# Linear attention: squares move from VectorE to ScalarE, the maxima are taken per half, and ScalarE's order in the queries' pass is new

## The reference

```python
def softmax_kernel_features(data, proj, is_query):
    d = data.shape[-1]
    data_normalizer = 1.0 / math.sqrt(math.sqrt(d))
    ratio = 1.0 / math.sqrt(proj.shape[0])
    data_dash = jnp.einsum('bhnd,md->bhnm', data_normalizer * data, proj)
    diag_data = jnp.sum(jnp.square(data), axis=-1, keepdims=True) * 0.5 * data_normalizer * data_normalizer
    if is_query:
        stab = jnp.max(data_dash, axis=-1, keepdims=True)
    else:
        stab = jnp.max(data_dash)
    return ratio * (jnp.exp(data_dash - diag_data - stab) + EPS)
...
q1 = softmax_kernel_features(q, proj_mat, is_query=True)
k1 = softmax_kernel_features(k, proj_mat, is_query=False)
kv = jnp.einsum('bhnm,bhnd->bhmd', k1, v)
ksum = jnp.sum(k1, axis=2)
z = 1.0 / jnp.einsum('bhnm,bhm->bhn', q1, ksum)
out = jnp.einsum('bhnm,bhmd->bhnd', q1, kv) * z[..., None]
```

## Time and profile before

| | us |
|---|---|
| Median of 3 runs | 2392.24 |
| Lowest and highest | 2391.66, 2395.35 |
| The profiled execution: its span, from the first to the last instruction | 2403.1 |
| TensorE busy in it | 1879.3 (78%) |
| VectorE busy | 1495.5 (62%) |
| ScalarE busy | 1074.7 (45%) |
| Keys' pass, first transposes to last VectorE pass | 147.2 to 255.1 |
| Queries' pass, first products to last VectorE pass | 330.6 to 529.1 |

### The profile page before, as it was taken

One profiled execution on the slowest core, in us unless ns is written; L12 is line 12 of the kernel. 1 busy time (PEld: TensorE's weight loads), 2 busy tenths in 40 slices (PEclk: granted clock), 3 DMA queues, 4 the chain that ended last, 5 costly groups with the idle time before them and its releaser, 6 DMA issues. The chain is left out here.

```text
span 2403.1 us, 30974 instructions
## 1 busy us (share of the span) xinstructions
PE 1879.3 (78%) x9780; PEld 1007.5 (42%) x9804; DVE 1495.5 (62%) x2518; ACT 1074.7 (45%) x1896; POOL 395.9 (16%) x595
## 2 busy tenths in 40 slices
PE   3868788858876453777668877998899984999994
PEld 2745655535333320000022234442133333888883
DVE  4558449966010687999878876999788883111114
ACT  1100222214110476999979964342477661222220
POOL 5000000000112010222100003331033343222221
PEclk8989999968887575555589978997799996999997
DMA  3011110005797004443011008777666703566664
GB/s 85 1 39 31 48 31 27 20 10 229 309 411 314 20 0 127 127 127 123 18 32 40 26 16 119 130 132 107 83 88 95 97 28 135 195 201 203 202 203 184
DMA packets 147792, 264.98 MB, mean 110 GB/s; under 512 B 28864, under 2 KB 115985, under 8 KB 142678
## 3 DMA queue, kind: packets, MB, share of 16 engines
q1 hardware_dynamic: 135750, 242.10, 38.0%
q0 software_dynamic: 10768, 18.19, 2.3%
q10 hardware_dynamic: 1152, 3.15, 0.3%
HBM read 221.85 MB, written 57.71 MB: 116 GB/s over the span
## 5 line engine op out<-in xcount | busy, mean ns | idle before, releaser
L1743 PE MATMUL ps<-arena 128*128 x376 | 194.9, 621 | 108.2 <-ACT ps L1785 60.1
L1785 ACT ACTIVATE ps<-ps,arena 128x512 f32<-128x512 f32 x384 | 256.7, 1121 | 6.3 <-POOL arena L1769 6.3
L1753 DVE TENSOR_REDUCE arena<-ps 128x1024 f32 x192 | 232.8, 1225 | 24.5 <-PE ps L1743 12.2
L1785 ACT ACTIVATION_READ_ACCUMULATOR ps<-ps,arena 128x1 f32 x384 | 234.7, 668 | 0.0
L2159 DVE TENSOR_REDUCE arena<-ps 128x1024 f32 x192 | 221.3, 1219 | 12.4 <-PE ps L2405 9.8
L2618 ACT ACTIVATE arena<-ps 128x1024 f32<-128x1024 f32 x192 | 185.1, 1020 | 97.6 <-PE ps L2500 96.4
L2962 DVE TENSOR_TENSOR arena<-ps,arena 128x384 f32<-128x384 f32 x39 | 21.8, 558 | 286.4 <-PE ps L2918 286.4
L2942 ACT ACTIVATE arena<-ps,arena 128x256 f32<-128x256 f32 x234 | 89.5, 481 | 235.9 <-PE ps L2907 230.0
L2405 PE MATMUL ps<-arena 96*128 96x512 bf16 x500 | 162.7, 430 | 26.4 <-DVE arena L2159 12.2
L1950 ACT ACTIVATE arena<-ps 128x1024 f32<-128x1024 f32 x192 | 178.7, 1048 | 7.8 <-DVE arena L1970 4.6
L529 PE MATMUL ps<-arena 96*128 96x456 f32 (+1 forms) x512 | 170.3, 482 | 8.8 <-DMA arena<-la_xt 5.2
(11 more groups left out here) (394 smaller groups left out, 3264.8 us busy)
## 6 DMA issues: line engine op xcount, KB each, us to landing
arena<-in_sm_w_dram SPq DMA_DIRECT2D x128, 576.0 KB, 15.5
arena<-in_re_w_dram SPq DMA_DIRECT2D x39, 1252.0 KB, 5.9
arena<-ra_parts SPq DMA_DIRECT2D x192, 192.0 KB, 9.1
routed_in<-routed_in SPq DMA_DIRECT2D x8, 3332.0 KB, 14.2
ra_parts<-arena SPq DMA_DIRECT2D x48, 192.0 KB, 2.4
arena<-routed_in SPq DMA_DIRECT2D x39, 196.0 KB, 5.4
arena<-la_xt SPq DMA_DIRECT2D x16, 384.0 KB, 3.4
arena<-arena SPq DMA_DIRECT2D x64, 96.0 KB, 2.2
```

The source lines that it names most:

```text
L1743: ins = pe.matmul(ps[:, 2 * (n % 4) + t % 2, :], QM[j][:, h, t * P:(t + 1) * P], KI[:, b, h // HG, :], start=True, stop=True)
L1753: v.tensor_reduce(MXq[:, b, 2 * u:2 * u + 2, at_head(h)], ps[:, 2 * (n % 4):2 * (n % 4) + 2, :], AX.X, ALU.max).then_inc(s_lk, 1)
L1785: ins = act.activation(bank, bank, ACT.Exp, bias=nb[n % 4][:, t % 2:t % 2 + 1], scale=c_reg, accum_out=RS[:, b, t, at_head(h):at_head(h) + 1])
```

## The change

VectorE's copy and product are left out in both passes. ScalarE squares the 192 numbers straight from PSUM into `SQ` (`square`), and VectorE sums what it wrote. A semaphore per pass (`ks`, `qs`) tells VectorE that the square is there. The maximum is taken in two instructions, one for each bank: first over bank 1, then, after the wait for the square, over bank 0 from which ScalarE reads the 192 numbers. In the keys' pass ScalarE's list is now squares of tiles 0 and 1, the copy of the next batch's turned rows, squares of tiles 2 and 3. In the queries' pass it is rewritten: square of t, exponential of t-1, copy of t-1. Before, it had the exponential of t and then the copy of t-1. TensorE's and SyncE's lists are as before.

```diff
-    MX = g2(P, [B, T])
+    MX = g2(P, [B, T, 2])
...
+    def square(act, b, t, product, done):
+        product.wait(act, b, t + 1)
+        act.activation(SQ[t % 2], ps[:, 2 * (t % 2), 0:D], ACT.Square).then_inc(done.sem, 1)
+
     def squared_lengths(v, link, t):
-        q = ps[:, 2 * (t % 2), 0:D]
-        link(v.tensor_copy(SQ[t % 2], q))
-        link(v.tensor_tensor(SQ[t % 2], SQ[t % 2], q, ALU.mult))
         link(v.tensor_reduce(dg[t % 2], SQ[t % 2].rearrange("p (h d) -> p h d", h=NH), AX.X, ALU.add))
+    one_group = lambda t, g: ps[:, 2 * (t % 2) + g, D:D + FH]
...
                 for t in range(T):
                     kp.wait(v, b, t + 1)
+                    largest = lambda g: v.tensor_reduce(MX[:, bass.ds(b, 1), t, g], one_group(t, g), AX.X, ALU.max)
+                    largest(1)
+                    ks.wait(v, b, t + 1)
+                    largest(0)
                     squared_lengths(v, link, t)
-                    v.tensor_reduce(MX[:, bass.ds(b, 1), t], features(t), AX.XYZ, ALU.max)
...
+            turned(0, 0, 0)
+            with act.Fori(0, B // 2 - 1) as i:
                 for j in range(2):
-                    b = 2 * i + j
-                    xt.wait(act, b, 1)
-                    prev(act, kp, i, j)
-                    act.wait_ge(s_xs[j], 16 * i + 1)
-                    act.activation(XTs[j], ps[0:DC, 4:6, :], ACT.Copy).then_inc(xc.sem, 1)
+                    squares(2 * i + j, (0, 1))
+                    turned(2 * i + j + 1, i + j, 1 - j)
+                    squares(2 * i + j, (2, 3))
...
                 qp.wait(v, b, t + 1)
-                q = ps[:, 2 * j, 0:D]
-                v.tensor_copy(SQ[j], q)
-                link(v.tensor_reduce(mq[j].rearrange("p (g h) -> p g h", g=2), features(t), AX.X, ALU.max))
-                link(v.tensor_tensor(SQ[j], SQ[j], q, ALU.mult))
-                link(v.tensor_reduce(dg[j], SQ[j].rearrange("p (h d) -> p h d", h=NH), AX.X, ALU.add))
+                largest = lambda g: v.tensor_reduce(mq[j][:, 6 * g:6 * g + 6],
+                                                    one_group(t, g).rearrange("p (h f) -> p h f", h=6), AX.X, ALU.max)
+                largest(1)
+                qs.wait(v, b, t + 1)
+                largest(0)
+                squared_lengths(v, link, t)
...
+            def batch(b, i, j, behind):
+                square(act, b, 0, qp, qs)
+                if behind:
+                    exp(b - 1, T - 1)
+                    turned(b - 1, 1 - j, T - 1)
+                prev(act, num, i, j)
+                for t in range(1, T):
+                    square(act, b, t, qp, qs)
+                    exp(b, t - 1)
+                    turned(b, j, t - 1)
```

More of the change, by code:

```diff
@@ L545, in linear_attention @@
         S1("k_products", T, T + 1), S1("k_features", T, 2)
+    ks = S1("k_squares", T, 2)
     s_lk, s_mx, s_gm, s_ns = (sem(f"la_{n}") for n in ("k_chain", "row_max", "global_max", "guard_ready"))
@@ L563, in batch @@
             def batch(b, ahead):
-                link = Link(v, s_lk, b * (3 * T))
+                link = Link(v, s_lk, b * T)
                 for t in range(T):
                     kp.wait(v, b, t + 1)
+                    largest = lambda g: v.tensor_reduce(MX[:, bass.ds(b, 1), t, g], one_group(t, g), AX.X, ALU.max)
+                    largest(1)
+                    ks.wait(v, b, t + 1)
+                    largest(0)
                     squared_lengths(v, link, t)
-                    v.tensor_reduce(MX[:, bass.ds(b, 1), t], features(t), AX.XYZ, ALU.max)
                     v.scalar_tensor_tensor(
@@ L580, in _ @@
             kd.wait(v, B - 1, T)
-            v.tensor_reduce(gmax, MX, AX.XY, ALU.max).then_inc(s_mx, 1)
+            v.tensor_reduce(gmax, MX, AX.XYZ, ALU.max).then_inc(s_mx, 1)
             v.wait_ge(s_gm, 1)
@@ L592, in _, with turned, squares @@
             xc.start(act)
+            ks.start(act)
             for j in range(2):
                 act.sem_inc(s_xs[j], 1)
-            with act.Fori(0, B // 2) as i:
-                for j in range(2):
-                    b = 2 * i + j
-                    xt.wait(act, b, 1)
-                    prev(act, kp, i, j)
-                    act.wait_ge(s_xs[j], 16 * i + 1)
-                    act.activation(XTs[j], ps[0:DC, 4:6, :], ACT.Copy).then_inc(xc.sem, 1)
+            def turned(b, i, j):
+                xt.wait(act, b, 1)
+                prev(act, kp, i, j)
+                act.wait_ge(s_xs[j], 16 * i + 1)
+                act.activation(XTs[j], ps[0:DC, 4:6, :], ACT.Copy).then_inc(xc.sem, 1)
+            def squares(b, some):
+                for t in some:
+                    square(act, b, t, kp, ks)
+            turned(0, 0, 0)
+            with act.Fori(0, B // 2 - 1) as i:
+                for j in range(2):
+                    squares(2 * i + j, (0, 1))
+                    turned(2 * i + j + 1, i + j, 1 - j)
+                    squares(2 * i + j, (2, 3))
+            squares(B - 2, (0, 1))
+            turned(B - 1, B // 2 - 1, 1)
+            squares(B - 2, (2, 3))
+            squares(B - 1, range(T))
         @block.sync
@@ L771, in linear_attention @@
         S1("q_turned", T, 2), S1("q_turned_copied", T, 2)
+    qs = S1("q_squares", T, 2)
     num, ot, pr, hh = S1("read_out", 2, 3), S1("normalised", 2), S1("projected"), S1("stream_updated")
@@ L826, in batch @@
             def batch(b, behind, last_behind):
-                link = Link(v, s_qk, b * (4 * T))
+                link = Link(v, s_qk, b * (2 * T))
                 chain(b, link, 0)
@@ L849, in _, with exp, turned @@
         def _(act):
-            for s in (qe, qc):
+            for s in (qe, qc, qs):
                 s.start(act)
-            with act.Fori(0, B // 2) as i:
-                for j in range(2):
[L854 to L864, removed]
+            def exp(b, t):
+                qd.wait(act, b, t + 1)
+                act.activation(QD[t % 2], QD[t % 2], ACT.Exp).then_inc(qe.sem, 1)
+            def turned(b, j, t):
+                qt.wait(act, b, t + 1)
+                act.activation(Q1T[j][:, :, t * P:(t + 1) * P].rearrange("p (g a) q -> p g a q", g=2),
+                               ps[0:2 * NF, 4:6, 0:3 * P].rearrange("p g (a q) -> p g a q", a=3),
+                               ACT.Identity, bias=little[0:2 * NF]).then_inc(qc.sem, 1)
+            def batch(b, i, j, behind):
[8 more added lines that the diff above has]
+                    turned(b, j, t - 1)
+            batch(0, 0, 0, False)
+            batch(1, 0, 1, True)
+            with act.Fori(1, B // 2) as i:
+                for j in range(2):
+                    batch(2 * i + j, i, j, True)
+            exp(B - 1, T - 1)
+            turned(B - 1, 1, T - 1)
         @block.tensor
```

## The result

The changed kernel takes 2382.8 us (median of 7 runs, 2379.4 to 2386.9) beside 2392.7 us for the kernel before (7 runs): ratio 0.9949, 95% interval 0.9937 to 0.9962. By the medians it is faster by 9.9 us, where 9.1 were forecast; by the ratio, which takes in all runs, it is 12 us (9 to 15). In two later groups of runs, on two chips, the same kernel stood at 0.9932 (0.9909 to 0.9956) and 0.9932 (0.9909 to 0.9954), which is 16 us by the ratio and 17.0 and 17.7 us by the medians. The three intervals overlap, so it is not shown that the gain differs from group to group. The forecast held in the comparison for which it was made; what the traces show that it did not have comes further down.

A forecast was written before the change was run, and what follows sets the result against it. A chain between TensorE and VectorE bounds the keys' round, VectorE the queries' pass. Gains of 8.2 us (keys) and 0.9 us (queries) sum to 9.1, from a median of 2392.24 to 2383.1 us; 8 in 10 range 2377.5 to 2391.

The forecast's parts named there:

- The chain: Keys' pass: links between TensorE and VectorE set the round, 12.73 us before and 11.71 us after.
- VectorE's 1.95 us: Keys' pass: VectorE's work on a tile, from data to the next instruction, falls from 2.52 to 1.95 us.
- the product's 2.46 us: Keys' pass: TensorE's time for one product, 2.46 us, half of L529's 5.00 without its last drain of 0.08.
- the round of 11.71: Keys' pass: 5.84 + 2.62 + 1.95 + 1.30 = 11.71 us a round, 1.02 less than 12.73.
- The wait of 1.12 us: Queries' pass: TensorE waits 1.12 us, twice a round, before transposes of tiles 1 and 3, for square and exponential.
- VectorE's 2.2 us of relief: Queries' pass: VectorE loses 0.71 us per tile and gains 0.15, about 2.2 us of its 19.94 a round.
- 1.0 in all: End of the queries' pass: VectorE's last two tiles are shorter by 0.5 us each, 1.0 us in all.
- rival c: Queries' pass: TensorE's clock falls and the kernel is slower, a round costing up to 19 us more; 9 in 100.
- no other stage changes: Outside the two passes: no other stage changes; one moving by more than 2 us would show the prediction wrong.
- (a): Both passes: squares come late, keys' gain only 5.6 us, queries' pass loses 2.5 or more, 2389 to 2391 us; 18 in 100.
- (b): Queries' pass: TensorE's two new waits don't appear, rounds fall towards 19 to 20 us, another 10 us, 2374; 5 in 100.
- (d): Keys' pass: TensorE's rate or something outside sets the round, so the gain stays under 4 us; 8 in 100.

The follow-up runs named there:

- e5: Changed kernel with the next batch's rows normalised at the start of a batch of the keys' pass, not after tile 0; 2350.4 us, ratio 0.9899.
- e6: Changed kernel with one maximum over both banks again, after the wait for the square, in both passes; 2373.8 us, ratio 0.9989.
- e4: Changed kernel with the exponential of tile t-1 ahead of the square of tile t in ScalarE's queries' list; 2357.9 us, ratio 0.9900.
- e8: Kernel before with four extra unread TensorE products ahead of batch 7's last transposes and four ahead of batch 6's projection; ratio 1.0004.
- e2: Changed kernel with the queries' pass as in the kernel before, so only the keys' pass is changed; ratio 0.9949.
- e3: Changed kernel with the keys' pass as in the kernel before, so only the queries' pass is changed; ratio 0.9966.
- e7: Changed kernel with nine extra unread TensorE products in each of its two 4.2 us waits in batch 7 of the queries' pass; ratio 0.9953.
- e12: Changed kernel with the edits of e4, e5 and e7 together, on a third chip; 2355.1 us, ratio 0.9822 to the kernel before.
- e11: Changed kernel with the edits of e4 and e5 together, on a third chip; 2362.9 us, ratio 0.9853 to the kernel before.
- e1: Changed kernel run again with no edit, for a second trace; 2362.7 us, ratio 0.9932 to the kernel before.
- e10: Changed kernel run again with no edit on a third chip, for a third trace; 2381.3 us, ratio 0.9932 to the kernel before.
- e9: Kernel before run again on a third chip, for a second trace of it; 2399.5 us, ratio 1.0004.

## Why the prediction was right, and where it was not

**The keys' pass.** Forecast 8.2 us, measured 9.1. The chain, VectorE's 1.95 us (1.96), the product's 2.46 us (2.42) and the round of 11.71 (11.63) all held, and e5 and e6 moved it as the chain says: without the normalising in it 10.55 us, with the square uncovered 12.13. Of the 0.9 us by which the term is too small some 0.7 are the product's rate, 0.04 us each, twice in a round and five times in the end. The 1.95 us were a little lucky: the prediction's own steps for them add up to 2.01. Its 0.10 us for the release of the square did not come, since the sum over the heads starts 0.69 us behind the first half maximum (210.16 to 210.85), which is twice the 0.34 us of a half and next to nothing more.

**The queries' round.** Forecast 21.2 us, measured 21.19 and 21.26. The wait of 1.12 us stood twice (1.03 and 0.95), VectorE's 2.2 us of relief did not shorten the round beyond that, and the start of the pass lost 1.4 to 1.7 us (first landmark to first addition 46.2 us before, 47.5 to 47.8 after) where 1.6 was forecast. e4 shows the reason as forecast: with the order turned round, both waits go.

**The end of the queries' pass** is the step that was mis-sized. The prediction gave "1.0 in all" for VectorE's shorter last tiles. Measured from VectorE's sixth addition to its last (L819, L843), it is 5.6 us by the two first traces: 46.3 us before, 40.7 after (4.8 us by the second trace of the kernel before). Some 1.2 of that is outside the clock; the rest, 4.4, is the projection of batch 6, 2.72 us and not 5.36, and the read-out of batch 7, 1.92 and not 3.64. TensorE's timeline, first of the kernel before:

```profile
494.07 0.83 PE L875 MATMUL ps<-arena 128*88 128x128 f32 x6 [1.12 <-ACT arena L862]
496.76 0.83 PE L875 MATMUL ps<-arena 128*88 128x128 f32 x6 [1.86 <-ACT arena L862]
499.18 1.01 PE L898 MATMUL ps<-arena 128*128 128x192 f32 x2 [1.59 <-DVE arena L814]
...
505.81 3.64 PE L889 MATMUL ps<-arena 88*32 88x512 f32 x16 [1.14 <-DVE arena L819]
```

and then of the changed kernel:

```profile
485.31 0.86 PE L915 MATMUL ps<-arena 128*88 128x128 f32 x6 [1.52 <-ACT arena L879]
487.23 0.59 PE L938 MATMUL ps<-arena 128*128 128x192 f32 x2 [1.06 <-DVE arena L838]
...
491.25 1.92 PE L929 MATMUL ps<-arena 88*32 88x512 f32 x16 [1.14 <-DVE arena L843]
```

The waits ahead of the two are 1.52 and 1.06 us now, where the kernel before has 1.86 and 1.59 and a third of 1.12 us ahead of them. The prediction treated the clock only as a danger (rival c), and took the half clock of the earlier trace rows for a fixed price. It was not one: with shorter waits of TensorE, which come from VectorE's shorter tiles and ScalarE's new order together, the clock stays full in the traces. e8 shows it by filling two of the three waits in the old code. The waits are not all that decides: with the same ones e2 loses the full clock five pairs later than the kernel before. What the Trainium skill says of waits that come back in each iteration ("TensorE: Matmul & The Clock Gate", section on HAM oscillation) does not show in the rounds of either kernel, where the granted clock is 1.00; in this pass it fell only behind the waits of the last batch, and there the shorter waits worked in favour of the change.

**What the sum did not have at all** is the stretch in the mixture of experts, 79.5 and 80.2 us in the traces of the kernel before and 72.4 to 72.5 in three of the changed one. Busy time by stretch for the 20 us that end with its last landmark, first of the kernel before:

```profile
599.40:619.40 20.00, 18.41 (x98) 5.94 (x97) 0.69 (x3) 2.68 (x3) 0.00 (x0) 0.50 0.32 118
```

and then of the changed kernel:

```profile
575.70:595.70 20.00, 17.25 (x143) 7.74 (x141) 5.42 (x17) 5.42 (x9) 0.00 (x0) 0.91 0.15 48
```

In the one TensorE runs these 20 us at 0.50, in the other at 0.91 in the mean. Each of the fourteen traces has one of two values: 72.4 to 72.8 in those of the changed kernel and of e2, e3, e5, e7 and e12, 79.5 to 80.4 in those of the kernel before and of e4, e6, e8 and e11. The prediction had "no other stage changes", and named a move of over 2 us in another stage as a sign of being wrong; by that sign it failed here, in all three traces of the changed kernel. The change alone does not fix the value, though: e4 and e11 contain it with one or two moves more and have the long one. The times follow it on the whole. What a kernel gains beyond the gain of its two passes in the trace is 3 to 6 us for e1, e2, e3, e5, e10 and e12 (e1: 17.0 against 14.1), and -3 to -6 us for e4, e6 and e8 (e4: 21.7 against 27.1). Two don't fit: e7 has the short value and -7 us, e11 the long one and +2. For e7 the trace is not of a typical run: with the time of the traced execution (2357.5 us) the -7 becomes +1.5. And the stages further on vary too: from the first expert to the end, where all the kernels have the same code, the fourteen traces take 1776.2 to 1783.9 us; e11 has 1776.4 and e9, the kernel before on its chip, 1783.5.

In the first comparison 9.9 us came out (12 by the ratio) where the two passes have 14.1 in the traces, with the short value in the changed kernel's. So the size of the whole, 10 to 18 us by the medians, is made of 14 us in the passes, which the traces show, and of what TensorE's clock does later. That the first comparison came within 1 us of the forecast is luck in part: the passes gave 5 us more than the sum had, and the rest of the program took 4 back. What selects the value in the mixture, and how often each occurs without a trace, stays open.

**The rivals.** (a), late squares: no. VectorE does not wait for them (1.96 us from the data to the normalising); e6, where it waits on each tile, costs 4.7 us in the passes. (b), the queries' pass gains all: not in this kernel, but e4 shows that it was to be had with two lines exchanged. (c), the clock falls in the queries' rounds: 1.00 in all of them. (d), nothing moves: no.

**The split maximum.** The Trainium skill's rule against small instructions ("VectorE: DVE Perf Modes", section on the TRN2 errata), which it gives for operands in SBUF, would have it merged. The halves, which read PSUM, took 0.43 us each, as estimated, so the split does cost 0.15 us of VectorE's work, of which 0.06 are in the chain (0.77 us for both halves beside 0.71 for the whole). That is less than the wait that it covers: e6 without it is slower by 3.9 us in the keys' pass.

## What to carry to other kernels

When two engines hand tiles to and fro and neither is busy throughout, add up the links of one round from the timeline until they give the round exactly; the sum then says what each edit is worth, and here it did so to 0.1 us a round for the change and to 0.25 for the experiments. When work moves to an idle engine that has a fixed list, look at what in that list now waits for a later event than before: in the queries' pass two exchanged lines on ScalarE were worth 12.9 us in the trace, the change itself 5.0. And a stretch at half clock is not a constant: waits that become some tenths shorter may give back several us of TensorE work behind them, and a later stage may move with them either way. So look at the stages that an edit does not touch, too, and at whether the traced execution is a typical one.

## What the runs showed of the hardware

- A small reduction on VectorE over 264 numbers from PSUM takes 0.43 us beside ScalarE's square of 192 numbers from the neighbouring bank, and the same to 0.01 us without it; the square takes 0.33 us there as in e6, where VectorE waits for it. The two don't slow each other.
- TensorE's granted clock at the end of the pass: with waits of 1.12, 1.86 and 1.59 us shortly before, it was down in three of three traces (the kernel before twice, e2), twice from the first product of the projection and once from its sixth pair; with 1.52 and 1.06 us (1.40 in e6, 1.45 in e4, e11 and e12) it stayed in ten of ten. Behind the waits of 4.2 us it was down in all twelve traces that had them unfilled, in nine of which it had been full ahead of the first of them; nine extra products in each of them kept it (e7, e12).
- The same instructions of a later stage take 72.4 to 72.8 or 79.5 to 80.4 us, and the granted clock over its last 20 us goes with it in all fourteen traces (0.91 against 0.50). The kernel before had the long time in both of its traces and the changed kernel the short one in all three; programs that differ from them in the stage ahead had either. That one program has both is likely from the two sets of times of e4 and e7, but no trace shows it.
